# State-space layer: encoder product in three single passes, residual added by transfers, statistics and gates at other places

## The chip, the cores and the metric

One Trainium2 chip; the program runs on one of its cores. Its engines are TensorE (PE in the profile; PEld is its weight load), VectorE (DVE), ScalarE (ACT), GpSimd (POOL) and SyncE (SP), which here only issues transfers. The metric is the device time of one launch in microseconds: before the change 4286.31 us, the median of 3 runs (4282.78 to 4290.16).

## The reference

Four layers follow each other on x, 8 images of 384 channels by 32x32 points (1024 tokens). Each computes `x = x + layer(group_norm(x))`: attention, the state-space layer, a depthwise convolution, and a recurrent layer with a convolution. Only the second is changed. It computes, for each image:

```python
fx = layernorm(u, ln1_g, ln1_b)                   # u: group norm of x, tokens by channels
Bu = einsum('ph,blh->blp', B_bar, fx)             # complex, 192 states
xs = scan(lam_bar, Bu)                            # along the 1024 tokens
y  = 2*real(einsum('hp,blp->blh', Cc, xs)) + D*fx
y  = gelu(y) + fx
fy = layernorm(y, ln2_g, ln2_b)
z  = fy @ W_enc.T                                 # 384 -> 768, the encoder
z1, z2 = split(z)
y  = (z1 * gelu(z2)) @ W_dec.T + fy               # the decoder
x  = x + y
```

## The kernel before

`s5_layer` works on one image at a time, with the 384 channels as 3 tiles of 128 partitions and the 1024 tokens in two halves of 512 columns. Everything is float32. Its engines run three images deep: in turn `i` of the main loop they do the second layer norm, encoder and decoder of image `i`, the complex rotation, scan and back rotation of image `i+1`, and the group norm and first layer norm of image `i+2`. The order on each engine is the order in which its block is written (no planner), and engines meet at semaphores only. B is 8.

TensorE's order in a turn: group means of `i+2`; the products with `b_w` of `i+1` (18 matmuls of 128x128 by 128x512), between them the channel sums of the two layer norms (8 matmuls, `norm`); the second half of the decoder of image `i-1` (9); the encoder of `i` (`fill_enc`, L1515, 36); the first half of the decoder of `i` (L1526, 9); the products with `c_w` of `i+1` (`fill_c`, L1536, 18), which need the last of the nine rotations `turn_out` (L1362). All of these but the norm sums write into a ring of four PSUM banks (`ORDER`, `wait_for_bank`): a product waits until the reader of the product four places ahead has read. The encoder alternates a bank for gelu (read by ScalarE, `gates`, L1222) and a bank for the factor (read by VectorE, `apply_gate`, L1368, which multiplies it by the gate). So the fifth bank waits for gate 0, the sixth for `apply_gate(0)`, and so on; the ninth for gate 2.

VectorE in a turn, from the second layer norm's last step on: scale of `y` (`scale`, L853), end of the rotation `turn_in` (L1330 to L1334), second half of the outputs of image `i-1` (`outputs`: L1381 adds the decoder bank to `xres`, L1385 is its statistics), statistics of the input of image `i+3` (`moments`, L104), three scans (L1338) with the scale of `f` (L853) among them, nine `turn_out` (L1362), six `apply_gate` and two `add_residual` (L1373) among these, first half of the outputs of image `i`, then `activations` of `i+1` (L1411 and L1416), which take the banks of `c_w`.

ScalarE: the layer norm's gain and bias on `y` (`affine`, L1204), gates 0 and 1, gain and bias on `f` for image `i+2` (L1204 again), gates 2 to 5, the gelus of `activations`. GpSimd adds tiles for the first layer norm's sums (L1163 to L1171). `add_residual` adds the normalised `y` to `xres`, into which SP has loaded the layer's input of that image again (L1145); this load waits for the store of the image before from the same buffer.

A setup block ahead of the loop turns the weights by transposes on TensorE (L1064), which ScalarE copies out of PSUM (L976, L981, L984). All engines meet at its end, and the statistics of image 0 follow (L104).

Of the kernel before, what the change touches and what calls it, by code (L numbers as in the profile page):

```python
# [57 lines left out]
def as_f32(ap):  # L58
    return ap.bitcast(F32)
# [796 lines left out]
def s5_layer(nc, const, x_in, x_out, moments_out, w):  # L856
# [12 lines left out]
    with ExitStack() as ctx:  # L869
# [8 lines left out]
        enc_w = sb("enc_w", [P, CT, 2 * C])  # L878
# [7 lines left out]
        xres = sb("xres1", [P, CT, T])  # L886
        f1 = [sb(f"f1_{n}", [P, CT, T]) for n in range(2)]
        y = sb("y1", [P, CT, T])
        hid = sb("hid1", [P, CT, T])
# [10 lines left out]
        x_loaded, res_loaded, stored = (ctx.enter_context(nc.semaphore(n)) for n in ("x_loaded1", "res_loaded1", "stored1"))  # L900
# [11 lines left out]
        b_bar = flat(f1[0], 0, TILES * C).rearrange("p (k c) -> p k c", k=TILES)  # L912
        count, times, high, low, whole = u[:, 0, :].bitcast(mybir.dt.int32), u[:, 1, :], u[:, 2, :], u[:, 3, :], z[:, 0, :]
# [8 lines left out]
        with nc.cleanup_on_exit(), ExitStack() as setup:  # L922
            lam_loaded, b_loaded, c_loaded, w_loaded, params = (nc.alloc_semaphore(n) for n in (
                "lam_loaded", "b_loaded", "c_loaded", "w_loaded", "params"))
            counted, v, s, mixed, bar, turned, kept = (Signal(nc.alloc_semaphore(n)) for n in (
                "counted", "s5_v", "s5_s", "c_mixed", "b_barred", "turned1", "kept1"))
# [27 lines left out]
            def _(pool):  # L954
                pool.iota(count, pattern=[[1, T]], base=0, channel_multiplier=0).then_inc(counted.next(), 1)
                pool.wait_ge(c_loaded, 16)
                for part in range(2):
                    source = c_rows[:, :, 2 * P + part:2 * STATES:2]
                    pool.tensor_copy(c_mix[:, :, part * REST:(part + 1) * REST], source).then_inc(mixed.next(), 1)

            @block.scalar
            def _(act):
# [7 lines left out]
                for n in range(CT * 3 + TILES + CT):  # L970
                    act.wait_ge(turned.sem, turned.at(n + 1))
                    source = psum[:, n % RING, 0:C]
                    if n < CT * 3:
                        t, which = n // 3, n % 3
                        target = dec_w[:, t, :] if which == 2 else enc_w[:, t, which * C:(which + 1) * C]
# [104 lines left out]
        f_made = signal("f_made", 2 * CT)  # L1080
# [13 lines left out]
        res_added = signal("res_added", 2)  # L1094
# [35 lines left out]
        def _(sp):  # L1130
            def store(i):
                sp.wait_ge(out_made.sem, out_made.at(2 * CT, i))
                sp.dma_start(x_out[i:i + 1].rearrange("a (p t) n -> p (a t n)", t=CT), xres[:, :, :].rearrange("p t n -> p (t n)")).then_inc(stored, 16)

            for i in range(-3, B):
                if i == 0:
                    sp.dma_start(xres[:, :, :].rearrange("p t n -> p (t n)"), x_in[0:1].rearrange("a (p t) n -> p (a t n)", t=CT)).then_inc(res_loaded, 16)
# [36 lines left out]
        def _(act):  # L1174
# [49 lines left out]
            for i in range(-2, B):  # L1224
# [17 lines left out]
                if batch(i):  # L1242
                    gates(i, 0, 2)
# [1266 lines left out]
```

## Time and profile before

| | |
|---|---|
| median of the runs | 4286.31 us |
| the profiled execution | 4282.44 us |
| its span, first to last instruction | 4280.0 us |
| PE busy / DVE busy / ACT busy / POOL busy in the span | 91 / 72 / 53 / 32 % |
| one turn in the steady part of the layer (2265.30 to 2355.30 us) | 90.00 us |
| in that turn PE / DVE / ACT / POOL busy | 85.37 / 76.91 / 35.26 / 12.29 us |

The layer's setup begins at 1856.92 us and its last store is done by 2686.0 us. Times within the program are us from the start of the span. A row of the time line gives start, duration, engine, line, operation, tiles and count; a bracket at its end is the idle time ahead of it and who ended it. "fp32r" is the data type of the high and low parts with which TensorE does one pass over the moving columns; a float32 matmul appears as two instructions and is counted twice.

### The profile page before, as it was taken

The numbers are of one execution on the slowest core, as the hardware profiler recorded it, in microseconds if no ns is written. First come the engines' busy times: TensorE is split into PE (matmuls) and PEld (weight loads), VectorE is DVE, ScalarE is ACT, GpSimd is POOL, SyncE is SP. The second block draws the span as 40 slices with busy tenths as digits, with TensorE's granted clock in tenths as the row PEclk, the third lists the DMA queues.
The fourth block names the chain that finished last, engine by engine and source line by source line (L and its number), as shares of the span: only waits on it lengthen the run. The fifth ranks groups of instructions, "written<-read, shape, count | busy, mean of one in ns | idle before, by whom it ended". The sixth has DMA issues, their size and how long they took to land. (4 is left out here: it accounts for less than half of the span.)

```text
span 4280.0 us, 53507 instructions
## 1 busy us (share of the span) xinstructions
PE 3884.5 (91%) x17085; PEld 2311.0 (54%) x17085; DVE 3078.0 (72%) x3127; ACT 2283.8 (53%) x3634; POOL 1372.1 (32%) x1106
## 2 busy tenths in 40 slices
PE   6999999999999999946999999465999999999999
PEld 5777768686868677622444444243444444444444
DVE  4767676666767675557887885355878878878878
ACT  2867667676858585834433432212644644644644
POOL 2857666675757485822111100222000000000000
PEclk8999999999999999967999999687999999999999
DMA  4323333342423232221111111776010010010010
GB/s 125 84 85 96 98 88 106 81 111 74 115 79 104 79 105 73 54 76 49 54 49 50 49 53 46 195 207 203 4 44 16 29 44 16 28 44 16 28 44 15
DMA packets 115528, 312.07 MB, mean 73 GB/s; under 512 B 47890, under 2 KB 49506, under 8 KB 105586
## 3 DMA queue, kind: packets, MB, share of 16 engines
q1 hardware_dynamic: 106802, 276.75, 21.2%
q0 software_dynamic: 7504, 24.80, 2.3%
q10 hardware_dynamic: 1008, 7.67, 0.5%
q8 instruction: 134, 2.20, 0.2%
q14 instruction: 80, 0.66, 0.1%
HBM read 203.12 MB, written 101.30 MB: 71 GB/s over the span
## 5 line engine op out<-in xcount | busy, mean ns | idle before, releaser
L417 POOL TENSOR_TENSOR probs_lo<-probs,probs_hi 128x512 fp32r<-128x512 f32 x848 | 1169.4, 1394 | 639.7 <-ACT probs L463 618.5
L530 DVE TENSOR_REDUCE maxima<-m_psum 128x1 fp32r<-128x1024 f32 x512 | 625.5, 1222 | 371.7 <-PE m_psum L706 370.8
L462 ACT ACTIVATE probs_hi<-s_psum 128x512 fp32r<-128x512 f32 x1024 | 613.4, 599 | 383.5 <-PE o_psum L735 221.9
L2431 PE MATMUL psum<-mixes,last_weights 128*128 128x512 f32 x1728 | 751.2, 593 | 0.0
L463 ACT ACTIVATE probs<-s_psum 128x512 f32<-128x512 f32 x1024 | 609.0, 595 | 0.0
L2431 PEld LDWEIGHTS psum<-mixes,last_weights 128*128 128x128 f32 x1728 | 328.2, 190 | 409.1 <-issue 409.1
L719 PE MATMUL s_psum<-q_all,k_hi 128*128 128x512 f32 x1024 | 430.9, 421 | 26.0 <-ACT probs L463 25.7
L735 PE MATMUL o_psum<-probs_lo,v 128*112 128x512 f32 x1024 | 412.5, 403 | 12.6 <-DVE probs_lo L610 6.5
L720 PE MATMUL s_psum<-q_all,k_lo 128*128 128x512 f32 x1024 | 405.0, 396 | 0.0
L730 PE MATMUL o_psum<-probs_hi,v 128*112 128x512 f32 x1024 | 404.6, 395 | 0.0
L2438 PE MATMUL psum<-xp,last_weights 128*128 128x512 f32 x864 | 383.2, 597 | 18.4 <-DVEq L2315 13.3
L706 PE MATMUL m_psum<-k_hi,q_all 128*128 128x512 f32 x1024 | 342.8, 417 | 31.2 <-DVE maxima L530 18.0
L706 PEld LDWEIGHTS m_psum<-k_hi,q_all 128*128 128x128 f32 x1024 | 289.3, 324 | 73.7 <-DVE maxima L530 26.3
L2438 PEld LDWEIGHTS psum<-xp,last_weights 128*128 128x128 f32 x864 | 161.9, 189 | 233.7 <-issue 207.4
L1515 PE MATMUL psum<-y,enc_w 128*128 128x512 f32 x576 | 253.6, 600 | 13.2 <-DVE hid L1368 13.2
L719 PEld LDWEIGHTS s_psum<-q_all,k_hi 128*128 128x128 f32 x1024 | 195.7, 191 | 120.9 <-ACT probs L463 97.4
L1906 PE MATMUL psum<-xt,last_weights 32*32 32x248 f32 (+3 forms) x5376 | 134.3, 451 | 111.3 <-issue 79.9
L735 PEld LDWEIGHTS o_psum<-probs_lo,v 128*112 128x112 f32 x1024 | 180.2, 176 | 88.6 <-POOL probs_lo L417 21.2
L720 PEld LDWEIGHTS s_psum<-q_all,k_lo 128*128 128x128 f32 x1024 | 194.4, 190 | 25.7
L610 DVE TENSOR_TENSOR probs_lo<-probs,probs_hi 128x512 fp32r<-128x512 f32 x176 | 193.0, 1097 | 20.1 <-ACT probs L463 18.8
L730 PEld LDWEIGHTS o_psum<-probs_hi,v 128*112 128x112 f32 x1024 | 180.0, 176 | 45.4
L1515 PEld LDWEIGHTS psum<-y,enc_w 128*128 128x128 f32 x576 | 110.3, 193 | 155.9 <-issue 132.6
(329 smaller groups left out, 5941.0 us busy)
## 6 DMA issues: line engine op xcount, KB each, us to landing
xin<-x SPq DMA_DIRECT2D x17, 1536.0 KB, 6.7
xin<-in_x SPq DMA_DIRECT2D x16, 1536.0 KB, 7.4
k_hi<-k_rows_hi SPq DMA_DIRECT2D x128, 192.0 KB, 3.4
xres<-x SPq DMA_DIRECT2D x16, 1536.0 KB, 7.2
k_rows_hi<-stage_hi SPq DMA_DIRECT2D x48, 256.0 KB, 2.1
k_rows_lo<-stage_lo SPq DMA_DIRECT2D x48, 256.0 KB, 2.3
q_rows_hi<-stage_hi SPq DMA_DIRECT2D x48, 256.0 KB, 2.4
q_rows_lo<-stage_lo SPq DMA_DIRECT2D x48, 256.0 KB, 2.5
```

The costliest lines, as they stand in the source:

```text
L417: pool.tensor_tensor(probs_lo[:, u % RING, :], probs[:, u % RING, :], as_f32(probs_hi[:, u % RING, :]), ALU.subtract).then_inc(pool_low.ne ...
L462: nc.scalar.activation(probs_hi[:, u % RING, :], s_psum[:, u % 2, :], ACT.Exp, scale=SCALE)
L463: nc.scalar.activation(probs[:, u % RING, :], s_psum[:, u % 2, :], ACT.Exp, scale=SCALE).then_inc(exped.next(), 1)
L530: nc.vector.tensor_reduce(maxima[:, g % 2, tile:tile + 1], source, AX.X, ALU.max, negate=True).then_inc(rows_max.next(), 1)
L706: ins = nc.tensor.matmul(pair_of(other)[:, half, :], q_all[:, g % SLOTS, tile::KEYS], k_hi[:, g % SLOTS, cols_of(half)], start=True, stop= ...
L719: nc.tensor.matmul(s_psum[:, u % 2, :], k_hi[:, h % SLOTS, keys], q, start=True, stop=False)
L720: nc.tensor.matmul(s_psum[:, u % 2, :], k_lo[:, h % SLOTS, keys], q, start=False, stop=True).then_inc(scored.next(), 1)
L730: nc.tensor.matmul(o_psum[0:USED, half, :], v[:, tile, h, :], probs_hi[:, u % RING, :], start=(tile == 0), stop=False)
L735: nc.tensor.matmul(o_psum[0:USED, half, :], v[:, tile, h, :], probs_lo[:, u % RING, :], start=False, stop=(tile == KEYS - 1)).then_inc(wei ...
L1515: ins = nc.tensor.matmul(bank("enc", i, 2 * n + k), enc_w[:, t, first + m * P:first + (m + 1) * P], y[:, t, cols(half)], start=(t == 0), s ...
L2431: ins = nc.tensor.matmul(bank, conv_w[:, t, down, factor, m * P:(m + 1) * P], mixes[:, factor, t, down:down + S, :].rearrange("p a b -> p ...
L2438: ins = nc.tensor.matmul(bank.rearrange("p (a b) -> p a b", b=S), weights[:, t, m * P:(m + 1) * P], rows_of(t, half), start=(t == 0), stop ...
```

## The change

Three things are done in `s5_layer`, and nothing elsewhere.

The encoder's operands are split. In the setup GpSimd makes from the turned weights a high part (a copy that rounds to fp32r) and a low part (the difference), six pieces of 128x384 each. For each image ScalarE writes gain and bias of `y` into `y_hi` (`highs`, in place of the first `affine`), and `y_lo` is the difference of the full value and `y_hi` (`lows`, VectorE). The full value itself is written into `residuals[i % 2]`: half 0 by VectorE, half 1 by ScalarE (`wholes`). Each float32 matmul of the encoder becomes three fp32r ones: high by high, low weights by high, high weights by low.

The residual has two buffers now. The load of the layer's input into `xres` and both `add_residual` are gone; GpSimd, once all of `y_lo` is made, issues three transfers that add the input of the image onto the full value in SBUF, and `outputs` waits for them.

The order is another: the six statistics of the next input image are spread over the first three `outputs` and the first three `activations`, with their total behind; the six `apply_gate` stand between other instructions than before.

```diff
+                for t in range(CT):
+                    for which in range(2):
+                        at = enc_turned[:, t, which * C:(which + 1) * C]
+                        high, low = (w_part[:, t, which * C:(which + 1) * C] for w_part in (enc_hi, enc_lo))
+                        pool.wait_ge(kept.sem, kept.at(3 * t + which + 1))
+                        pool.tensor_copy(high, at).then_inc(enc_split.next(), 1)
+                        pool.wait_ge(enc_split.sem, enc_split.at(enc_split.count))
+                        pool.tensor_tensor(low, at, as_f32(high), ALU.subtract).then_inc(enc_split.next(), 1)
...
-                    sp.wait_ge(out_measured.sem, out_measured.at(1, i - 1))
-                    sp.wait_ge(stored, 16 * i)
-                    sp.dma_start(xres[:, :, :].rearrange("p t n -> p (t n)"), x_in[i:i + 1].rearrange("a (p t) n -> p (a t n)", t=CT)).then_inc(res_loaded, 16)
...
+                if batch(i):
+                    pool.wait_ge(low_made.sem, low_made.at(2 * CT, i))
+                    for t in range(CT):
+                        pool.dma_start(residuals[i % 2][:, t, :], x_in[i].rearrange("(p t) n -> p t n", t=CT)[:, t, :],
+                                       accum_op=ALU.add).then_inc(res_added, 16)
...
+            def wholes(i):
...
+                for t in range(CT):
+                    nc.scalar.activation(residuals[i % 2][:, t, cols(1)], y[:, t, cols(1)], ACT.Identity,
+                                         scale=rows["ln2_g"][:, t:t + 1], bias=rows["ln2_b"][:, t:t + 1]).then_inc(f_second_half.next(), 1)
...
-                    affine(y, rows["ln2_g"], rows["ln2_b"], scaled2, f_made, i)
+                    highs(i)
...
-                    gates(i, 0, 2)
+                    gates(i, 0, 1)
+                    wholes(i)
+                    gates(i, 1, 2)
...
+            def lows(i, half):
+                whole = residuals[i % 2]
+                if half == 0:
...
+                    for t in range(CT):
+                        nc.vector.tensor_scalar(whole[:, t, cols(0)], y[:, t, cols(0)], rows["ln2_g"][:, t:t + 1], rows["ln2_b"][:, t:t + 1],
+                                                ALU.mult, ALU.add).then_inc(f_first_half.next(), 1)
+                for t in range(CT):
...
+                    dve.wait_ge(high_made.sem, high_made.at(nth, i))
+                    nc.vector.tensor_tensor(y_lo[:, t, cols(half)], whole[:, t, cols(half)], as_f32(y_hi[:, t, cols(half)]),
+                                            ALU.subtract).then_inc(low_made.next(), 1)
...
                         for t in range(CT):
-                            ins = nc.tensor.matmul(bank("enc", i, 2 * n + k), enc_w[:, t, first + m * P:first + (m + 1) * P],
-                                                   y[:, t, cols(half)], start=(t == 0), stop=(t == CT - 1))
+                            for w_part in (enc_hi, enc_lo):
+                                nc.tensor.matmul(bank("enc", i, 2 * n + k), w_part[:, t, at], y_hi[:, t, cols(half)],
+                                                 start=(t == 0 and w_part is enc_hi), stop=False)
+                        for t in range(CT):
+                            if m == 0 and k == 0:
+                                pe.wait_ge(low_made.sem, low_made.at(CT * half + t + 1, i))
+                            ins = nc.tensor.matmul(bank("enc", i, 2 * n + k), enc_hi[:, t, at], y_lo[:, t, cols(half)],
+                                                   start=False, stop=(t == CT - 1))
```

VectorE in a steady turn, from the outputs of the image before to the third gate; `hid` is `apply_gate`, `z<-decay,u` a scan. Before:

```order
668 L1393 SCALAR_TENSOR_TENSOR x_moments<-x_moments 128x1
669 L104 BN_STATS gn_stats<-xin 128x6 x6
...
672 L1338 SCALAR_TENSOR_TENSOR z<-decay,u 128x1024
673 L853 TENSOR_TENSOR f_1<-f_1,ln_inv 128x3x512 x2
674 L1368 TENSOR_TENSOR hid<-gate,psum 128x512
675 L1338 SCALAR_TENSOR_TENSOR z<-decay,u 128x1024 x2
676 L1368 TENSOR_TENSOR hid<-gate,psum 128x512
```

And now:

```order
764 L1449 SCALAR_TENSOR_TENSOR x_moments<-x_moments 128x1
765 L1425 TENSOR_TENSOR hid<-gate,psum 128x512
766 L1395 SCALAR_TENSOR_TENSOR z<-decay,u 128x1024
767 L1333 TENSOR_TENSOR y_lo<-xres_0,y_hi 128x512 x3
768 L1425 TENSOR_TENSOR hid<-gate,psum 128x512
769 L853 TENSOR_TENSOR f_0<-f_0,ln_inv 128x3x512 x2
770 L1425 TENSOR_TENSOR hid<-gate,psum 128x512
771 L1395 SCALAR_TENSOR_TENSOR z<-decay,u 128x1024
```

The statistics are gone from here, the first gate stands ahead of the first scan, and the third stands directly behind the scale of `f` instead of behind two more scans and four rotations.

ScalarE at the same place; `y_hi` and `y` are gain and bias of the second norm, `f` those of the first. Before:

```order
814 L1204 ACTIVATE y<-y,ln_b_c,ln_g_c 128x512 x6
...
817 L1222 ACT_TABLE_LOAD
818 L1222 ACTIVATE gate<-psum 128x512 x2
819 L1204 ACTIVATE f_1<-f_1,ln_b_c,ln_g_c 128x512 x6
820 L1222 ACTIVATE gate<-psum 128x512 x4
```

And now:

```order
835 L1228 ACTIVATE y_hi<-y,ln_b_c,ln_g_c 128x512 x6
...
839 L1254 ACTIVATE gate<-psum 128x512
840 L1236 ACTIVATE xres_0<-y,ln_b_c,ln_g_c 128x512 x3
841 L1254 ACTIVATE gate<-psum 128x512
842 L1219 ACTIVATE f_0<-f_0,ln_b_c,ln_g_c 128x512 x6
843 L1254 ACTIVATE gate<-psum 128x512 x4
```

Three activations stand between the first two gates; the third gate is behind the six of `f`, as before.

## Rows read from the trace of the kernel before

**Rows 1.** Windows, one steady turn: us; PE, PEld, DVE, ACT, POOL; PEclk, DMA, GB/s.

```profile
2265.30:2355.30 90.00, 85.37 (x201) 37.27 (x199) 76.91 (x93) 35.26 (x47) 12.29 (x8) 1.00 0.16 59
```

**Rows 2.** Time line of PE in that turn, from encoder to c_w products.

```profile
2297.10 13.04 PE L1515 MATMUL psum<-y,enc_w 128*128 128x512 f32 x30
2312.84 15.72 PE L1515 MATMUL psum<-y,enc_w 128*128 128x512 f32 x36 [2.70 <-DVE hid L1368]
2329.34 2.84 PE L1515 MATMUL psum<-y,enc_w 128*128 128x512 f32 x6 [0.78 <-DVE hid L1368]
2332.02 7.89 PE L1526 MATMUL psum<-hid,dec_w 128*128 128x512 f32 x18
2339.75 15.61 PE L1536 MATMUL psum<-u,c_w 128*128 128x512 f32 x36
```

**Rows 3.** Time line of PE in the attention layer: fp32r matmuls, one each.

```profile
1002.15 0.39 PE L720 MATMUL s_psum<-q_all,k_lo 128*128 128x512 f32 x1
1002.37 0.39 PE L730 MATMUL o_psum<-probs_hi,v 128*112 128x512 f32 x1
```

**Rows 4.** Time line of DVE in the turn of rows 1.

```profile
2291.31 4.97 DVE L853 TENSOR_TENSOR y<-y,ln_inv 128x1536 f32<-128x1536 f32 x2
2296.20 0.68 DVE L1330 TENSOR_TENSOR prod<-u,tables 128x512 f32<-128x512 f32 x1
2298.01 1.27 DVE L1381 TENSOR_TENSOR xres<-xres,psum 128x512 f32<-128x512 f32 x2
2302.30 3.65 DVE L104 BATCH_NORM_STATS2 gn_stats<-xin 128x6 f32<-128x512 f32 x6
2308.79 3.40 DVE L853 TENSOR_TENSOR f<-f,ln_inv 128x1536 f32<-128x1536 f32 x2
2312.11 0.68 DVE L1368 TENSOR_TENSOR hid<-gate,psum 128x512 f32<-128x512 f32 x1
2312.70 4.47 DVE L1338 TENSOR_TENSOR_SCAN z<-decay,u 128x1024 f32<-128x1024 f32 x2
2327.47 1.23 DVE L1362 TENSOR_TENSOR u<-u 128x1024 f32<-128x1024 f32 x1
2328.61 0.68 DVE L1368 TENSOR_TENSOR hid<-gate,psum 128x512 f32<-128x512 f32 x1
```

**Rows 5.** Time line of ACT in the same turn.

```profile
2310.56 4.34 ACT L1204 ACTIVATE f<-f,ln_b_c,ln_g_c 128x512 f32<-128x512 f32 x6 [4.93 <-DVE f L853]
2314.80 0.57 ACT L1222 ACTIVATE gate<-psum 128x512 f32<-128x512 f32 x1
```

**Rows 6.** Time line of DVE: a tensor_scalar while it builds its tables.

```profile
1896.28 0.69 DVE L1298 TENSOR_SCALAR u<-u 128x1024 f32<-128x1024 f32 x1
```

**Rows 7.** Time line of PE: encoder and c_w products of images 5 and 7.

```profile
2476.99 31.06 PE L1515 MATMUL psum<-y,enc_w 128*128 128x512 f32 x72
2515.61 15.61 PE L1536 MATMUL psum<-u,c_w 128*128 128x512 f32 x36
2633.35 31.06 PE L1515 MATMUL psum<-y,enc_w 128*128 128x512 f32 x72
```

**Rows 8.** Time line at the end of the setup.

```profile
1871.80 1.10 POOL L959 COPY xres<-xres 128x192 f32<-128x192 f32 x2 [13.88 <-DMA xres<-in_L_conv_Cmat]
1875.65 1.24 ACT L984 COPY b_w<-psum 128x384 f32<-128x384 f32 x3 [0.96 <-PE psum L1064]
1878.41 3.66 DVE L104 BATCH_NORM_STATS2 gn_stats<-xin 128x6 f32<-128x512 f32 x6 [3.53 <-PEq L922]
```

**Rows 9.** Groups of the page and of POOL: busy us, mean ns, idle ahead.

```profile
L610 DVE TENSOR_TENSOR probs_lo<-probs,probs_hi 128x512 fp32r<-128x512 f32 x176 | 193.0, 1097 | 20.1 <-ACT probs L463 18.8
L1163 POOL TENSOR_TENSOR first_sums<-f 128x512 f32<-128x512 f32 x16 | 21.3, 1329 | 439.3 <-ACT f L1182 439.3
```

**Rows 10.** Page, part 6: issues, KB each, median us to landing.

```profile
xres<-x SPq DMA_DIRECT2D x16, 1536.0 KB, 7.2
dw_res<-x POOLq DMA_DIRECT2D x96, 128.0 KB, 4.1
```

More of the change, by code:

```diff
@@ L877, in s5_layer @@
         c_w = sb("c_w", [P, TILES, C])
-        enc_w = sb("enc_w", [P, CT, 2 * C])
+        enc_hi, enc_lo = (sb(f"enc_w_{part}", [P, CT, 2 * C], F32R) for part in ("hi", "lo"))
         dec_w = sb("dec_w", [P, CT, C])
@@ L974, in _ @@
                         t, which = n // 3, n % 3
-                        target = dec_w[:, t, :] if which == 2 else enc_w[:, t, which * C:(which + 1) * C]
+                        target = dec_w[:, t, :] if which == 2 else enc_turned[:, t, which * C:(which + 1) * C]
                         nc.scalar.copy(target, source).then_inc(kept.next(), 1)
@@ L1407, in activations @@
                 for n in range(2 * CT + 2):
+                    if i >= 1 and batch(i + 2):
+                        if n < CT:
+                            measure(i + 2, CT + n)
+                        if n == CT + 1:
+                            moments(i + 2)
                     if n < 2 * CT:
@@ L1436, in _, with scale_and_split @@
                     table(1)
-                scale_second = (lambda: scale(norm2, y, inv_made2, scaled2, i)) if here else None
+                def scale_and_split():
+                    scale(norm2, y, inv_made2, scaled2, i)
+                    lows(i, 0)
+                scale_second = scale_and_split if here else None
                 if after:
@@ L1443, in _ @@
                     outputs(i - 1, EARLY, 2 * CT)
-                if batch(i + 3):
+                if batch(i + 3) and not here:
+                    for n in range(2 * CT):
+                        measure(i + 3, n)
                     moments(i + 3)
+                if here:
+                    apply_gate(i, 0)
                 if after:
                     scan(i + 1, 0)
+                if here:
+                    lows(i, 1)
+                    apply_gate(i, 1)
                 if third:
@@ L1450, in _ @@
                 if here:
-                    apply_gate(i, 0)
+                    apply_gate(i, 2)
                 if after:
                     scan(i + 1, 1)
+                if here:
+                    apply_gate(i, 3)
+                if after:
                     scan(i + 1, 2)
-                if here:
-                    apply_gate(i, 1)
-                if after:
-                    for n in range(4):
+                    for n in range(2):
                         turn_out(i + 1, n)
                 if here:
-                    apply_gate(i, 2)
+                    apply_gate(i, 4)
+                if after:
+                    for n in range(2, 4):
+                        turn_out(i + 1, n)
+                if here:
+                    apply_gate(i, 5)
                 if after:
```

67 lines of the change are left out of this document (45 added, 22 removed).

## The prediction

> **What bounds the kernel now.** I read the windows of the layer first, then the time lines of TensorE, VectorE and ScalarE in one turn, and last the rows of the setup. A steady turn lasts 90.0 us; TensorE is busy for 85.37 of it at full clock, VectorE for 76.91, ScalarE for 35.26 [rows 1]. TensorE is the bound, with 5 us of gaps, of which 2.70 and 0.78 are waits in the encoder for `apply_gate` on VectorE [rows 2]. So two things could shorten a turn: less work on TensorE, and gates that come earlier. VectorE is only 8.5 us behind and gets more work, so I follow both engines through the turn until the products with `c_w` start (2339.75 us before). These need the last rotation of VectorE, and what follows them is as before. The turn is shorter by what this start gains.
>
> **TensorE's part.** The encoder's 36 float32 matmuls are 72 instructions, 31.06 us where nothing waits [rows 7], so 0.863 us for each matmul. Now there are 108 fp32r ones. In the attention layer these start 0.22 to 0.23 us apart, each with its own weights [rows 3]; with 0.231 the encoder takes 24.95 us, 6.1 less. This is a size that the trace shows for the same kind of operation, so I keep its other bounds narrow: 0.215 to 0.25, 23.2 to 27 us. After it come 9 decoder matmuls, 7.73 us (2332.02 to 2339.75, [rows 2]). From the start of the encoder, 2297.10, TensorE alone would reach the `c_w` products after 33 us at 2330, against 2339.75.
>
> **VectorE's part.** I count from the end of the scale of `y`, 2296.20 [rows 4], in the new order. An operation on 128x512 takes 0.59 us from start to start (2312.11 to 2312.70), a rotation 1.14 (2327.47 to 2328.61), a scan 2.2 (4.47 for two), the scale of `f` 3.35, the second half of the outputs with its total 4.3 (2298.01 to 2302.30) [rows 4]. A `tensor_scalar` on 128x1024 takes 0.69 [rows 6], so three on 512 about 1.2.
>
> Low parts of half 0: 1.2 + 3x0.6 + 0.1 for waiting on itself = 3.1, to 2299.3. End of `turn_in` 1.8, outputs 4.3, gate 0 0.6, scan 2.2, low parts of half 1 1.8, gate 1 0.6, scale of `f` 3.35: 2313.95. Now gate 2 is due, and there is the new wait. ScalarE makes this gate behind its six activations on `f`, and these wait for the scale of `f`. Before, the scale ended at 2312.1 (VectorE went on at 2312.11) and the gate at 2315.4 [rows 4, 5]: 3.3 us later, which nobody felt, since `apply_gate(2)` came far behind. It now stands directly behind the scale, so VectorE waits 3.3 us, to 2317.25. Queued behind it are all that follows: gate 2 0.6, scan 2.2, gate 3 0.6, scan 2.2, two rotations 2.27, gate 4 0.6, two rotations 2.27, gate 5 0.6, five rotations 5.75. The last rotation ends at 2334.35.
>
> TensorE beside it: its first low-part matmul waits until 2298.1, the third until 2299.3, which costs 0.3; the ninth bank needs gate 2, is due at 2314.1 and starts at 2317.4, 3.3 us lost; the others find their gates done, since gate 0 (2306.0) and gate 1 (2310.7) are now ahead of the banks that need them (2308.4 and 2312). The 2.70 and 0.78 of before are gone. The encoder ends at 2325.6, the decoder's half at 2333.4, and TensorE waits a microsecond for the rotation. So the start is 2334.35 instead of 2339.75: **5.4 us per steady turn**, set by VectorE. This holds for images 1 to 4: 21.6 us.
>
> The statistics (six times 0.61, before all in one piece of 3.65 and with their total 4.3 us [rows 4]) cost nothing at their new place: three lie among the first outputs and three in `activations`. From 2334.35 VectorE has 9 operations (5.4 us), then 3 statistics, the total, five products and the sums, together 14.2 us in the 15.61 us of the `c_w` products. Beyond 1.4 us more the next turn would begin late by the rest. The two additions of the residual (2 x 1.67 us between the last gates) are gone as well; they are simply not in the new chain.
>
> **The other images.** Image 0 has no earlier outputs (4.3 less on VectorE), image 6 no scale of `f` and no wait for gate 2 (6.65 less): there TensorE is the bound and gains about 5.9 each. Image 7 has nothing behind its encoder but the decoder: 6.0. Image 5 had no input statistics before, so its encoder ran without a wait, 38.62 us from its start to the `c_w` products [rows 7]; the new chain is the same as above, 37.25 us, gain 1.4. Together 21.6 + 11.8 + 6.0 + 1.4 = 40.8 us.
>
> **The setup.** GpSimd was done with two copies at 1872.9, and the block ended with `b_w` at 1876.9; the statistics start 1.5 later [rows 8]. Now GpSimd has twelve more instructions on 128x384 that start at 1872.9, because the weights come out earlier. A subtraction on 128x512 takes 1.33 us on it [rows 9], so 0.97 on 384. A copy isn't shown in this size: 0.55 for 192 columns [rows 8] gives 0.55 at least and 1.1 at most. I take 0.8, between them, and 0.1 for each of the twelve waits: 6x(0.97 + 0.8) + 1.2 = 11.8, end 1884.7, **8 us late**, all on the path, since every engine meets there. Bounds 6 and 10.
>
> **The transfers.** The old load of 1536 KB took 7.2 us from issue to landing [rows 10]; it and its wait for the store go and nothing was waiting there. The new ones start when the low parts are complete (2310.0) and are wanted at 2334.35: 24.3 us. No row shows a transfer that adds. From below: as a plain one, 7 us, hidden. From above: three times that, 21.6, still hidden in a steady turn; image 6 has only 17.7 us (4 us lost), image 7 some 20.7. I take it as hidden, nearest to the plain row; GpSimd has nothing else to do behind the issue until the next turn.
>
> The Trainium skill, "SBUF — State Buffer", section "SBUF: two separate sides", says that a transfer issued by GpSimd stands still while VectorE runs an operation that takes both of its ports, because GpSimd can't write the descriptors; "Who interferes with whom" there names `tensor_scalar` as such and `tensor_tensor` as not. By that the new issue would be undisturbed, as the only `tensor_scalar` of a turn lie 12 us ahead of it; if the rule held for the other operations too, the issue would wait up to one of them. No run here shows it yet.
>
> **Sum.** 4282.44 - 40.8 + 8 = 4249.6 for the profiled execution; this one lay 3.9 us under the median, so 4253.5 as a median, 32.7 us or 0.8% faster.
>
> **Rivals.**
> 1. *No wait at gate 2.* If ScalarE has the gate early, VectorE reaches the last rotation at 2331.05, TensorE is at 2330.2, and the turn gains 8.7: 34.8 for four images, 4.7 for image 5, 17.8 for the rest, less 8: 4237. For it: 35 of 90 us busy on ScalarE. Against it: its order, in which gate 2 follows the activations on `f`.
> 2. *VectorE pays more for the low parts.* The same kind of subtraction has a mean of 1097 ns in the attention layer, where GpSimd works beside it [rows 9], instead of 0.6. Six of them cost 3 us a turn, and image 1 to 5 lose that from the chain, 15 us: 4269. Against it: GpSimd is idle in this stretch.
> 3. *Transfers that land late* (the other side). VectorE stands at the first output, and TensorE behind it as its banks stay full. With landing L after the last low part, six images lose L - 24.3, image 6 L - 17.7 and image 7 L - 20.7. The 32.7 us are used up at L = 27.1, nearly four times the plain load; at 30 us the loss is 55.8 and the kernel takes 4309. For it: an adding transfer has to read its target, and rows of such a kind are missing. Against it: it would have to go at 50 KB/us where the plain load goes at 213.
> 4. *The gain is eaten.* Setup 10 instead of 8, fp32r matmuls at 0.25, low parts dearer and 4 us lost at image 6: 4280, no measurable change.
>
> **Chances.** My forecast with its own spread (4246 to 4262) 0.55, rival 1 0.12, rival 2 0.14, rival 3 0.07, rival 4 0.12, of which a part is still faster. What a measurement of this kernel can tell from no change is about 0.2%, 8.6 us: faster means under 4277.7. That gives 0.85 faster (0.55, 0.12, 0.14 and a third of rival 4's), 0.08 the same, 0.07 slower. Range 4236 to 4280: from rival 1 to rival 4, all but rival 3 and a little at either end.
>
> **What would show it.** In the new profile: the encoder's fp32r matmuls 0.23 us apart; a wait of VectorE of about 3.3 us for gate 2, released by ScalarE, and TensorE's wait of the same size in front of the ninth bank; turns of 84.6 us; `c_w` products that wait about a microsecond for a rotation; GpSimd's copies and subtractions to 1885 and the statistics of image 0 at about 1886.4; no wait of VectorE for a transfer at the first output. A turn of 81 would speak for rival 1, a turn of 88 or subtractions of over 0.7 for rival 2, an idle time ahead of the first output released by a DMA for rival 3.

## The result and the profile after

The changed kernel took 4251.73 us (median of 4 runs, 4245.56 to 4256.85) beside 4288.21 us for the kernel before (4 runs): a ratio of 0.9919, 95% interval 0.9906 to 0.9933 (the medians divided by each other give 0.9915). The forecast was 4253.5, in a range of 4236 to 4280. The profiled execution took 4248.17 us with a span of 4246.4, against 4282.44 and 4280.0.

To see where the time went I use two marks that both traces have: the start of a row of `c_w` products (once a turn), and the whole distance of the layer from the first GpSimd instruction of its setup (an IOTA) to the first matmul on `x_moments` behind its last image. First these marks in the trace after; columns: start in us, busy us, engine, line, operation, tiles, count, and in brackets the idle time ahead with what ended it.

```profile
1858.75 0.98 POOL L961 IOTA u<- 128x1024 int32 x1 [27.41 <-POOLq L181]
1986.48 17.10 PE L1615 MATMUL psum<-u,c_w 128*128 128x512 f32 x36 [19.75 <-DVE u L1419]
...
2241.06 15.72 PE L1615 MATMUL psum<-u,c_w 128*128 128x512 f32 x36 [1.00 <-DVE u L1419]
2326.43 15.72 PE L1615 MATMUL psum<-u,c_w 128*128 128x512 f32 x36 [1.00 <-DVE u L1419]
2411.79 15.72 PE L1615 MATMUL psum<-u,c_w 128*128 128x512 f32 x36 [1.01 <-DVE u L1419]
2497.13 15.72 PE L1615 MATMUL psum<-u,c_w 128*128 128x512 f32 x36 [1.01 <-DVE u L1419]
2573.42 15.61 PE L1615 MATMUL psum<-u,c_w 128*128 128x512 f32 x36
...
2657.08 0.58 PE L1968 MATMUL psum<-x_moments,group_mean 128*128 128x16 f32 x2 [6.20 <-PEq L869]
```

The layer takes 2657.08 - 1858.75 = 798.3 us. Before, its marks stood at 1856.94 and 2686.12, 829.2 us. So it gained **30.9 us**; the prediction had 40.8 - 8 = 32.8. The rest of the program, which the change doesn't touch, took 3450.8 us in the trace before and 3448.1 in the trace after. Over all twelve profiled executions of this case it lies between 3448.1 and 3456.2 with no visible relation to the kernel. So single times here differ by some microseconds for reasons outside the layer, the medians lie 36.5 us apart where the layer gained 30.9, and part of the closeness of 4251.7 to 4253.5 is luck of that kind. Below, each term is judged by the marks.

The marks have a spread too, as each kernel has one trace. From the IOTA to the first `c_w` products the seven kernels that split the weights in the setup have as good as the same code and take 127.7 to 129.3 us. The first `c_w` products stand behind a wait of some 20 us, TensorE does part of them at its lower clock, and they take 17.1 to 18.8 us over the twelve kernels. So layers that differ by 3 us or less are told apart by their turns, which repeat within 0.15 us, and not by the whole distance.

A steady turn is now 85.37 us. Windows of it (us; busy time and count of PE, PEld, DVE, ACT, POOL; granted clock; DMA share; GB/s), which answers to [rows 1]:

```profile
2241.06:2326.43 85.37, 81.17 (x235) 44.83 (x235) 78.13 (x100) 37.27 (x50) 14.90 (x11) 0.98 0.22 62
```

TensorE is busy 4.2 us less than in [rows 1], not 6.1, and its clock is no longer whole. The time line of VectorE in this turn, which answers to [rows 4]:

```profile
2282.67 4.97 DVE L853 TENSOR_TENSOR y<-y,ln_inv 128x1536 f32<-128x1536 f32 x2
2287.56 1.45 DVE L1324 TENSOR_SCALAR xres<-y,ln_g_c,ln_b_c 128x512 f32<-128x512 f32 x3
2288.93 1.88 DVE L1333 TENSOR_TENSOR y_lo<-xres,y_hi 128x512 fp32r<-128x512 f32 x3
...
2292.55 1.27 DVE L1435 TENSOR_TENSOR xres<-xres,psum 128x512 f32<-128x512 f32 x2
...
2297.20 0.69 DVE L1425 TENSOR_TENSOR hid<-gate,psum 128x512 f32<-128x512 f32 x1 [0.28 <-PE psum L1594]
...
2302.39 3.42 DVE L853 TENSOR_TENSOR f<-f,ln_inv 128x1536 f32<-128x1536 f32 x2
2309.04 0.69 DVE L1425 TENSOR_TENSOR hid<-gate,psum 128x512 f32<-128x512 f32 x1 [3.23 <-ACT gate L1254]
...
2325.15 1.22 DVE L1419 TENSOR_TENSOR u<-u 128x1024 f32<-128x1024 f32 x1
2326.29 0.68 DVE L1435 TENSOR_TENSOR xres<-xres,psum 128x512 f32<-128x512 f32 x1
```

The wait at gate 2 is there, 3.23 us, and ScalarE releases it. The first output at 2326.29 waits for no transfer. ScalarE shows why the gate comes so late, as in [rows 5]: its six activations on `f` run first.

```profile
2304.18 4.35 ACT L1219 ACTIVATE f<-f,ln_b_c,ln_g_c 128x512 f32<-128x512 f32 x6 [4.38 <-DVE f L853]
2308.43 1.06 ACT L1254 ACTIVATE gate<-psum 128x512 f32<-128x512 f32 x2
```

And TensorE, which answers to [rows 2]:

```profile
2289.84 1.53 PE L1594 MATMUL psum<-y_lo,enc_w_hi 128*128 128x512 f32 x3
2293.27 0.79 PE L1589 MATMUL psum<-y_hi,enc_w_hi 128*128 128x512 f32 x1 [1.90 <-DVE xres L1435]
2293.86 0.63 PE L1589 MATMUL psum<-y_hi,enc_w_lo 128*128 128x512 f32 x1
2294.29 0.63 PE L1589 MATMUL psum<-y_hi,enc_w_hi 128*128 128x512 f32 x1
...
2297.16 0.40 PE L1589 MATMUL psum<-y_hi,enc_w_lo 128*128 128x512 f32 x1
2297.40 0.39 PE L1589 MATMUL psum<-y_hi,enc_w_hi 128*128 128x512 f32 x1
```

Here stand two things that the prediction did not have. In front of the second encoder bank TensorE waits 1.90 us for VectorE's addition of an output (L1435): this bank is the one that the decoder of the image before still holds, and the addition that frees it now stands behind the low parts: 5.0 us behind the end of the scale of `y`, where it stood 1.8 behind it [rows 4]. And behind this wait the fp32r matmuls start 0.43 us apart instead of 0.23, until 2296.9: the granted clock is 0.73 over the 6 us from 2293.27, so the engine runs at its lower level (1.2 GHz) for part of them.

The setup, which answers to [rows 8]:

```profile
1873.45 1.00 POOL L965 COPY xres<-xres 128x192 f32<-128x192 f32 x2 [13.72 <-DMA xres<-in_L_conv_Cmat]
1874.40 0.65 POOL L971 CAST enc_w_hi<-z 128x384 fp32r<-128x384 f32 x1
1875.13 1.18 POOL L973 TENSOR_TENSOR enc_w_lo<-z,enc_w_hi 128x384 fp32r<-128x384 f32 x1
...
1882.68 0.50 POOL L971 CAST enc_w_hi<-z 128x384 fp32r<-128x384 f32 x1
1883.26 0.99 POOL L973 TENSOR_TENSOR enc_w_lo<-z,enc_w_hi 128x384 fp32r<-128x384 f32 x1
1885.11 3.66 DVE L104 BATCH_NORM_STATS2 gn_stats<-xin 128x6 f32<-128x512 f32 x6 [7.80 <-PEq L928]
```

From the IOTA to the first statistics it is 26.36 us against 21.47 before: 4.9 us, not 8.

### The profile page after: what moved, and what is told of

It reads as the page before. It is cut to its first block and busy times, and to the rows that moved or that the text cites. A ratio compares the mean times of both kernels' runs of the same rounds, so it can differ in the third digit from the quotient of the medians.

```text
span 4246.4 us, 54195 instructions
## 1 busy us (share of the span) xinstructions
PE 3846.9 (91%) x17373; PEld 2366.5 (56%) x17373; DVE 3092.6 (73%) x3183; ACT 2300.1 (54%) x3658; POOL 1402.0 (33%) x1142
## 5 line engine op out<-in xcount | busy, mean ns | idle before, releaser
L706 PE MATMUL m_psum<-k_hi,q_all 128*128 128x512 f32 x1024 | 343.1, 417 | 30.9 <-DVE maxima L530 18.1
L1985 PE MATMUL psum<-xt,last_weights 32*32 32x240 f32 (+3 forms) x5376 | 136.1, 456 | 108.3 <-issue 74.5
L610 DVE TENSOR_TENSOR probs_lo<-probs,probs_hi 128x512 fp32r<-128x512 f32 x176 | 193.2, 1098 | 20.1 <-ACT probs L463 18.8
L1985 PEld LDWEIGHTS psum<-xt,last_weights 32*32 32x32 f32 x5376 | 95.2, 115 | 148.9 <-issue 97.9
L790 PE MATMUL m_psum<-heads,proj_w 128*128 128x512 f32 x384 | 166.8, 594 | 8.7 <-DVE v L536 8.7
```

The lines of the kernel that those rows point to most:

```text
L706: ins = nc.tensor.matmul(pair_of(other)[:, half, :], q_all[:, g % SLOTS, tile::KEYS], k_hi[:, g % SLOTS, cols_of(half)], start=True, stop= ...
L1985: ins = nc.tensor.matmul(out[:, :, rows], bands[q * S:(q + 1) * S, g, channel, tap, 0:S], xt[q * S:(q + 1) * S, t % 2, g * GROUP + channel ...
```

## The experiments

Ten kernels ran, in three groups; each group has its own runs of the kernel before (4284.92 us for the first four, 4285.14 for the next four, 4287.44 for the last two), and the ratio is to these; that of the changed kernel is to 4288.21. "Layer" is the distance between the two marks above in the one profiled execution, which leaves out what varies elsewhere.

```
kernel                       median us  ratio to before [95%]      layer us  steady turn
before                                                             829.2     89.9
changed kernel               4251.73    0.9919 [0.9906, 0.9933]    798.3     85.4
order_only                   4269.50    0.9962 [0.9948, 0.9976]    817.7     86.6
split_only                   4310.16    1.0061 [1.0044, 1.0077]    857.5     96.0
two_pass                     4241.33    0.9892 [0.9875, 0.9908]    783.9     85.0
no_residual                  4250.91    0.9916 [0.9899, 0.9932]    800.0     85.4
gate2_early                  4237.50    0.9888 [0.9872, 0.9905]    785.8     82.6 or 84.2
add_early                    4248.25    0.9911 [0.9894, 0.9927]    796.7     85.2
late_split                   4246.29    0.9907 [0.9891, 0.9924]    792.8     85.0
both                         4233.41    0.9879 [0.9863, 0.9896]    779.6     82.2
best                         4230.45    0.9866 [0.9850, 0.9881]    775.0     82.2
best_stats                   4221.10    0.9848 [0.9834, 0.9861]    767.0     81.0
```

### The change in its parts

**order_only** is the kernel before with VectorE's new order alone: three statistics among the first outputs and three in `activations`, and gates 0 to 5 at their new places. It keeps the loaded residual, whose two additions move behind the last rotation. Of its edit, the first three gates:

```diff
+                if here:
+                    apply_gate(i, 0)
                 if after:
                     scan(i + 1, 0)
+                if here:
+                    apply_gate(i, 1)
...
                 if here:
-                    apply_gate(i, 0)
+                    apply_gate(i, 2)
```

> The kernel before with two parts of the change alone: the statistics of the next input spread over outputs and activations, and the six gates at their new places; float32 encoder, loaded residual (its two additions stand behind the last rotation). My theory: TensorE still takes 31.06 us for the encoder and 7.73 for the decoder's half, but waits for no gate any more, so a steady turn falls from 90.0 by the 3.5 us of waits to about 86.5, image 5 gains nothing, and the whole is 12 to 16 us faster than before (ratio about 0.997). VectorE will still wait some 3 us for gate 2 behind the activations on f, without a price, because TensorE is the later of the two. Rival: the order is worth nothing by itself and the gain is all the fp32r encoder's: turns of 90, ratio 1.000.

Turns of 86.56 us (`c_w` products at 2243.5, 2330.1 and 2416.7), TensorE busy for 85.07 of 86.60 us. The order takes the encoder's waits away, and TensorE, with its float32 encoder, is then the bound. That is 11.5 us of the layer (15.4 by the medians), and with 1.5 us of gaps left in a turn little more can come from the order alone. VectorE's wait for gate 2 is there as well, 3.21 us, and costs nothing, as expected.

**split_only** is the changed kernel with the old order (statistics in one piece, gate 0 behind the scale of `f`).

```diff
-                if here:
-                    apply_gate(i, 0)
                 if after:
                     scan(i + 1, 0)
                 if here:
                     lows(i, 1)
-                    apply_gate(i, 1)
...
                 if here:
-                    apply_gate(i, 2)
+                    apply_gate(i, 0)
```

> The changed kernel with the order of VectorE undone: statistics in one piece ahead of the first scan and the gates at their old places (low parts of half 1 behind the first scan); split encoder and adding transfers kept. My theory: VectorE's longer chain and late gates hold the encoder's banks, the encoder ends about 10 us later than in the changed kernel, and a steady turn takes 93 to 95 us, more than the 90.0 of before; the whole is 10 to 25 us slower than before (ratio 1.002 to 1.006). Rival: TensorE's saving of 6.1 us a turn counts whatever the order: turns of 84 to 86 and a ratio near 0.991.

Turns of 96.0 us, the layer 28.3 us slower than before, although its encoder matmuls are the faster ones. TensorE's time line shows where they stand:

```profile
2227.77 0.50 PE L1578 MATMUL psum<-y_hi,enc_w_hi 128*128 128x512 f32 x1 [1.91 <-DVE xres L1435]
...
2243.68 0.80 PE L1578 MATMUL psum<-y_hi,enc_w_hi 128*128 128x512 f32 x1 [7.39 <-DVE hid L1425]
```

A faster encoder fills its banks sooner and then waits 7.39 us for gate 0. That alone explains no loss against the kernel before. But the split also puts the low parts on VectorE ahead of this gate: it starts 20.9 us behind the end of the scale of `y`, where it started 15.9 behind it [rows 4], and these 5.0 us are most of the 6 by which the turn got longer. The turn is longer than the 93 to 95 us that I expected. So the two parts are not additive: -11.5 for the order, +28.3 for the split, together -30.9. The split needs the order; the order brings something by itself.

**two_pass** leaves out the product of the low part of the weights with the high part of `y`.

```diff
-                            for w_part in (enc_hi, enc_lo):
+                            for w_part in (enc_hi,):
```

> The changed kernel without the products of the weights' low part (they are left out of the encoder): 72 instead of 108 fp32r matmuls, 8.3 us less for TensorE per image. My theory: VectorE's chain sets the turn, so steady turns stay at 85.4 less at most 1, images 6 and 7 gain some 2 and 8, in all 10 to 16 us less than the changed kernel (ratio to before about 0.989). Rival: TensorE is the bound and the turn falls by 8.3: 60 us less (ratio 0.978).

A third of the encoder's work gone from TensorE, 8.3 us, and the steady turn is 0.4 us shorter. TensorE just waits longer, 3.80 us instead of nothing at gate 2:

```profile
2305.71 0.69 DVE L1425 TENSOR_TENSOR hid<-gate,psum 128x512 f32<-128x512 f32 x1 [3.22 <-ACT gate L1254]
2305.73 1.65 PE L1589 MATMUL psum<-y_hi,enc_w_hi 128*128 128x512 f32 x3 [3.80 <-ACT gate L1254]
...
2323.09 2.41 PE L1615 MATMUL psum<-u,c_w 128*128 128x512 f32 x5 [1.14 <-DVE u L1419]
```

Of the gain, 14.4 us of the layer, images 6 and 7 bring 4.3 and 8.3: there TensorE is the bound. This shows that VectorE's chain sets the steady turns of the changed kernel, as predicted.

**no_residual** leaves out the three accumulating transfers and VectorE's wait for them.

```diff
-                if batch(i):
-                    pool.wait_ge(low_made.sem, low_made.at(2 * CT, i))
-                    for t in range(CT):
-                        pool.dma_start(residuals[i % 2][:, t, :], ..., accum_op=ALU.add).then_inc(res_added, 16)
...
-                        if n == 0:
-                            dve.wait_ge(res_added, 16 * CT * (i + 1))
```

> The changed kernel without the three adding transfers and without the wait for them (the layer's input is left out of its output). Theory: they land 10 us after the low parts are complete, 14 us before they are wanted, and cost nothing: the time of the changed kernel within 3 us (ratio 0.992). Rival: their traffic slows the swap of the scans' third tile or GpSimd's port slows VectorE: over 5 us faster than the changed kernel.

4250.91 against 4251.73 us, the same turns to 0.05 us (the layers differ by 1.6 us the other way, 1.55 of it ahead of the first `c_w` products): the transfers are hidden. In the changed kernel they are issued behind the last low part and land in a median of 7.8 us (5.4 to 10.5 over the 24), while 24 us are there.

```profile
2302.17 2.63 POOL L1185 DMA_DIRECT2D xres<-x x3 [16.15 <-DVE y_lo L1333]
```

### The two waits

**gate2_early** puts ScalarE's gate 2 ahead of its six activations on `f`.

```diff
-                    gates(i, 1, 2)
+                    gates(i, 1, 3)
...
-                    gates(i, 2, 2 * CT)
+                    gates(i, 3, 2 * CT)
```

> Full computation. ScalarE evicts and activates gate 2 (index 2) of the image ahead of the six activations of f instead of behind them. My theory: of the 3.2 us that VectorE waits for that gate in each turn (2309.04 in the trace of the changed kernel), all but about 0.3 goes, but TensorE has lost time earlier in the turn (1.90 us waiting for the decoder bank before the second encoder bank, then 0.43 us instead of 0.22 per start for some microseconds) and is itself only 1.0 us ahead of its wait for u, so the scan chain can be pulled forward by at most about 1 us before the next turn's start is set by TensorE. Expected: turns 84.4 us against 85.4, about 4246 us, ratio to before 0.991, that is 3 to 7 us under the changed kernel. Rival (the wait at gate 2 is the only thing that bounds the turn): turns 82.5, about 4230 us. Rival (the wait only moves to another one of the VectorE chain): no change, 4252 us.

More than my theory gave: 785.8 us for the layer, 12.5 less than the changed kernel. The wait at gate 2 is down to 0.43 us, as expected:

```profile
2298.17 0.69 DVE L1425 TENSOR_TENSOR hid<-gate,psum 128x512 f32<-128x512 f32 x1 [0.43 <-ACT gate L1254]
```

But the turns come in two lengths, and the rows of the windows tell why:

```profile
2146.43:2230.64 84.21, 81.02 (x235) 45.06 (x234) 78.78 (x101) 37.28 (x50) 14.92 (x11) 0.98 0.23 63
2230.64:2313.27 82.63, 79.44 (x235) 43.90 (x234) 77.76 (x100) 37.39 (x50) 14.92 (x11) 1.00 0.23 64
2313.27:2395.91 82.64, 79.44 (x236) 43.89 (x235) 78.19 (x101) 37.40 (x50) 14.91 (x11) 1.00 0.23 64
2395.91:2480.11 84.20, 81.03 (x236) 45.02 (x234) 78.75 (x101) 37.27 (x50) 14.90 (x11) 0.98 0.18 44
```

In the turns of 84.2 us the granted clock is 0.98 and TensorE busy for 81.0 us, in those of 82.6 it is 1.00 and 79.4. The wait in front of the second encoder bank is in all of them. The time line of TensorE in a long and in a short turn:

```profile
2198.55 0.50 PE L1589 MATMUL psum<-y_hi,enc_w_hi 128*128 128x512 f32 x1 [1.90 <-DVE xres L1435]
...
2201.86 0.63 PE L1589 MATMUL psum<-y_hi,enc_w_lo 128*128 128x512 f32 x1
2202.28 0.63 PE L1589 MATMUL psum<-y_hi,enc_w_hi 128*128 128x512 f32 x1
...
2282.77 0.50 PE L1589 MATMUL psum<-y_hi,enc_w_hi 128*128 128x512 f32 x1 [1.90 <-DVE xres L1435]
2283.10 0.40 PE L1589 MATMUL psum<-y_hi,enc_w_lo 128*128 128x512 f32 x1
2283.34 0.40 PE L1589 MATMUL psum<-y_hi,enc_w_hi 128*128 128x512 f32 x1
```

My 84.4 is near what the turns take in which the clock falls, and the error was to take the fall for granted. The same wait of 1.90 us is followed by it in two of these four turns, and this costs 1.6 us. The second rival, that the wait at gate 2 alone bounds the turn (82.5 us), came out for the others.

**add_early** takes the other wait away: the output addition that frees the second encoder bank moves ahead of the low parts of half 0, the two others right behind them. Not shown: `outputs` skips the three there.

```diff
                     scale(norm2, y, inv_made2, scaled2, i)
+                    if batch(i - 1):
+                        add_output(i - 1, EARLY)
                     lows(i, 0)
+                    if batch(i - 1):
+                        for n in range(EARLY + 1, 2 * CT):
+                            add_output(i - 1, n)
```

> Full computation. VectorE's three early output additions of the image before stand one ahead of the low parts of y and two right behind the first half of them, so that the decoder bank which the second encoder bank takes is free sooner; gate 2 stays behind f's activations. My theory: the 1.90 us wait of TensorE at the second encoder bank goes, and with it most of the stretch at half clock (0.43 us a start instead of 0.22); but gate 2 still comes behind the activations of f, so VectorE's chain to u keeps its length and TensorE waits some 2.5 us at the ninth bank or ahead of the matmul on u. Expected: turns 85.2 to 85.6 us, 4250 us, ratio 0.9915. Rival (TensorE's lost time bounds the turn by itself): turns 82.5, about 4231 us. Rival (the additions ahead lengthen the chain by 0.4 to 1.2 us): turns 86.2, 4257 us.

The wait at the second bank is gone, and the turn stays at 85.2 us, since the wait for gate 2 stays. TensorE now has a wait of its own for the same gate, and the lower clock follows there:

```profile
2304.45 0.69 DVE L1425 TENSOR_TENSOR hid<-gate,psum 128x512 f32<-128x512 f32 x1 [3.22 <-ACT gate L1254]
2304.47 0.73 PE L1600 MATMUL psum<-y_hi,enc_w_hi 128*128 128x512 f32 x1 [2.30 <-ACT gate L1254]
2304.99 0.63 PE L1600 MATMUL psum<-y_hi,enc_w_lo 128*128 128x512 f32 x1
2305.42 0.63 PE L1600 MATMUL psum<-y_hi,enc_w_hi 128*128 128x512 f32 x1
```

The layer is only 1.6 us shorter, but images 6 and 7, where TensorE is the bound, gain 1.6 us each; the stretch up to the first `c_w` products and these products took longer here, within the spread given above.

**both** has the two edits.

> Full computation. Both edits: gate 2 ahead of the activations of f on ScalarE, and the early output additions spread around the low parts on VectorE. My theory: each of the two waits hides the other (3.2 us of VectorE at gate 2; 1.9 us plus the half-clock stretch of TensorE at the second encoder bank), so only together do they give their full time. Expected: turns 82.0 to 82.6 us against 85.4, six of them, about 4234 us, ratio 0.988. Rival (gains are additive, no hiding): the sum of the two single gains, thus 4244 us or more if each gives 1 to 4 us. Rival (something third is 1 us behind, such as ScalarE's evictions): turns 84, 4243 us.

Turns of 82.22 us and a layer of 779.6, 18.7 us less than the changed kernel, where the single edits give 12.5 and 1.6. From the second `c_w` products on, without the stretch that varies, it is 17.9 against 11.2 and 4.3: 2.4 more than their sum, and the two falls of the clock in gate2_early are 3.2 us. Neither engine waits inside the encoder for longer than 0.5 us, and the clock is whole in the steady turns:

```profile
2232.76:2314.98 82.22, 79.69 (x234) 43.80 (x234) 78.06 (x100) 37.16 (x50) 14.91 (x11) 1.00 0.23 64
```

My theory, that each wait hides the other, holds only one way. Taking away TensorE's wait alone gives nearly nothing, since VectorE sets the turn; taking away VectorE's alone gives most of it, up to where TensorE becomes the bound. What the second edit adds is 0.4 us in the turns with the full clock and 2.0 us in the others.

### The setup, and what beats both kernels

**late_split** makes the encoder weights' high and low parts in the main loop, by GpSimd beside the scan work of the first image, instead of in the setup. The turned weights lie in `residuals[1]` instead of `z` for it, and TensorE waits for the parts ahead of the first encoder.

```diff
+                if i == -1:
+                    pool.wait_ge(turned_out.sem, turned_out.at(TURNS_OUT, 0))
+                    for t in range(CT):
+                        ... (tensor_copy to enc_hi, tensor_tensor to enc_lo)
```

> Full computation. The encoder weights' high and low parts are made by GpSimd in the main loop, beside the scan work of the first image, instead of in the setup; nothing else changes. My theory: the setup's 4.9 us over the kernel before (IOTA to first statistics 26.36 against 21.47 us) goes and nothing in the loop waits for the split. Expected: about 4246.5 us, ratio 0.9905, turns still 85.4. Rival (GpSimd's twelve instructions, 9.9 us, slow VectorE or delay the residual transfers of that turn): gain under 2 us, 4250 us. Rival (the setup's longer distance is due to something else, such as the order of loads): no gain, 4252 us.

The first statistics start at 1879.30, 21.41 us behind the IOTA at 1857.89: the 4.9 us are gone, and the loop has room for the work. The two kernels below that have this edit show 21.4 us as well, and the seven with the split in the setup 26.4 to 27.7. The layer is 5.5 us shorter. Its first turn is 1.3 us longer (85.03 against 83.71), all of it in its first `c_w` products (18.44 against 17.10 us, the spread given above). Its other turns are 0.4 us shorter. TensorE has the same wait of 1.90 us at the second bank in them, but full clock behind it in four of the five, and in the other one the clock falls 1.3 us later than in the changed kernel. A steady turn and its second bank:

```profile
2235.76:2320.75 84.99, 79.98 (x235) 43.72 (x235) 78.04 (x100) 37.27 (x50) 14.89 (x11) 1.00 0.22 62
...
2287.97 0.50 PE L1593 MATMUL psum<-y_hi,enc_w_hi 128*128 128x512 f32 x1 [1.90 <-DVE xres L1437]
2288.31 0.39 PE L1593 MATMUL psum<-y_hi,enc_w_lo 128*128 128x512 f32 x1
```

So the second bank is full in time, and VectorE has no wait at gate 0 in any of them, where it waits 0.25 to 0.37 us in the changed kernel.

**best** is both with late_split.

> Full computation. Gate 2 ahead of the activations of f, early output additions spread around the low parts, and the encoder weights' split in the main loop. My theory: the three gains stand in different places (VectorE's wait at gate 2, TensorE's wait at the second encoder bank with the half-clock stretch behind it, the setup) and so add: turns 82.2 us as in the kernel with the two waits gone, and some 5 us less of setup. Expected 4228 us, ratio to before 0.9867. Rival (the split on GpSimd now stands in a turn that has no idle time left to hide it, 9.9 us): 4233 to 4238 us.

4230.45 us, 2.5 above what I wrote; the layer is 775.0 us, 4.6 below that of `both`, with the same turns. The setup's gain adds to the others, as it stands in a different place.

**best_stats** moves VectorE's three late statistics and their aggregate (2.4 us) from the place ahead of gate 0 to behind the last rotation; the edit is against the kernel `best`.

```diff
-                if batch(i - 1):
-                    outputs(i - 1, EARLY, 2 * CT)
...
+                if batch(i - 1):
+                    outputs(i - 1, EARLY, 2 * CT)
                 if here:
                     outputs(i, 0, early(i))
```

> Full computation. As the kernel above, and VectorE's three late statistics of the image before with their aggregate (2.4 us) stand behind the last rotation instead of ahead of the first gate. My theory: the 82.2 us turn is bounded by VectorE's chain to u; taking 2.4 us out of it gives back no more than TensorE's 0.9 us wait before the matmuls on u, less what the 2.4 us cost behind it, where the additions to y wait only 1.7 us in all for TensorE. Expected: turns 81.5 to 82.0 us, 4225 us. Rival (the chain alone counts): turns 79.8, 4213 us. Rival (the statistics now delay y and the sums behind it): turns 82.9, 4232 us.

4221.10 us, the fastest here: 1.5% under the kernel before. The turn is 81.03 us, 1.2 shorter: below the 81.5 to 82.0 that I expected, and a little more than the 0.9 us that TensorE had waited. The `c_w` products now start without a wait. TensorE waits 1.4 us in a turn (1.15 in the decoder's second half, 0.26 for a low part) and is the bound again:

```profile
2223.70 15.61 PE L1630 MATMUL psum<-u,c_w 128*128 128x512 f32 x36
2304.73 15.61 PE L1630 MATMUL psum<-u,c_w 128*128 128x512 f32 x36
```

## Why the prediction was right, and where not

*The mechanism of the steady turn held.* VectorE's chain sets the turn, as two_pass shows (8.3 us less work for TensorE shorten it by 0.4), with the wait for gate 2 in it (3.3 us predicted, 3.23 measured) and with `c_w` products that wait about a microsecond (1.00). The matmuls start 0.23 us apart where the clock is whole. The chain from the end of the scale of `y` to the end of the last rotation was to be 38.15 us and is 38.7 (2287.56 to 2326.29): the gate 0 wait of 0.28, 0.2 for three `tensor_scalar` of 0.46 rather than 0.4 each, and small change. TensorE starts 0.14 behind the rotation, and the stretch ahead of the scale is 0.1 longer (41.61 instead of 41.50). Together the turn is 85.37, not 84.6: 4.5, 5.2, 4.6 and 4.6 us for images 1 to 4 where 5.4 each were forecast, 2.7 us too much in all.

*The step that failed* is "TensorE beside it: its first low-part matmul waits until 2298.1 [...] the ninth bank needs gate 2, is due at 2314.1". I followed the encoder's banks to the gates that free them, and not to the outputs of the image before. The second bank waits 1.90 us for such an output, which the low parts had pushed back by 3.2 us. With the lower clock behind it this used up the time that TensorE would have waited at the ninth bank: no wait is left there. In the steady turn this costs little beyond the 0.28 us at gate 0, since VectorE's chain is as long: add_early, which takes the wait away, has turns of 85.2, and late_split, in whose steady turns the wait is there but the clock stays whole, 85.0. In image 6, where TensorE is the bound, it has its price: 1.23 us of wait in the trace, and a gain of 4.6 us instead of 5.9. There the clock stays whole (1.00).

*The other images.* Image 0 gained 5.5 (5.9 forecast), of which 0.8 us lie in its first `c_w` products (17.10 instead of 17.86 us), where it is the spread given above and not the change. Image 5 gained 0.6 (1.4), image 7 6.0 (6.0). With images 1 to 4 and image 6 that is 35.5 us for 40.8.

*The setup* was a term of the right kind and a wrong size: 8 forecast, 4.9 measured. A copy of 384 columns takes 0.50 to 0.65 us where I took 0.8, the twelve instructions 9.85 us instead of 11.8, and the statistics begin 0.86 us behind the block's last instruction, not 1.5. late_split shows that all of the 4.9 us came from them. This error (3.1 us) and those of the images (5.3) had opposite signs, and that the sum came out within 2 us of the layer's gain is luck.

*The transfers* are hidden, as no_residual shows by leaving them out. By the Trainium skill, "SBUF — State Buffer", section "SBUF: two separate sides", GpSimd can't write the descriptors of a transfer while VectorE runs an operation in a mode that takes both ports. The trace agrees as far as it goes: the three issues take 2.63 us beside the scale of `f`, a `tensor_tensor`, which the prediction took for none of these, and no less, 2.62 and 2.60 us, in images 6 and 7, where no such scale runs and VectorE is idle for more than half of the time. The `tensor_scalar` of the turn lie 13 us ahead, so the other half of the rule isn't tested here.

*The rivals.* Rival 1 (no wait at gate 2) is what gate2_early builds, and it comes to 4237.5 us where I had reckoned 4237, though with the smaller setup and the wait at the second bank, which I didn't know, in it. Rival 2 fell: a low part takes 0.6 us. Rival 3 fell with no_residual. In rival 4 one part was near: the image terms came out smaller, but the setup did too.

What stays open: why the clock falls behind the 1.90 us wait in all five turns of the changed kernel that have it, but only in two of five of gate2_early, and in one of five each of late_split and split_only.

## What to carry to other kernels

When a step moves in the order of an engine, follow everything that is pushed back by it to whoever waits for it, the banks that the image before still holds included: a bank has two users. A faster matmul pays only if the engine that empties its banks comes earlier as well, and the work that the faster form puts on that engine counts; here the split without the new order lost 28 us, and with it won 31. Once a turn is bound by a chain through three engines, read its waits in order and take away the one that the bounding engine itself shows (gate 2 on VectorE), then the next, until no engine but one waits; with the split out of the setup that was worth as much again as the change (31.4 us of the layer).

## What the runs showed of the hardware

Three accumulating transfers of 512 KB from GpSimd's queue land in 5.4 to 10.5 us each, side by side, where the plain one of 1536 KB took 7.2 [rows 10]. A copy from float32 to fp32r of 128x384 on GpSimd takes 0.50 to 0.65 us, hardly more than the copy of 192 columns (0.50 in the same trace); a subtraction of 128x384 takes 0.99 to 1.21, where I had 0.97 from one of 512 columns. An fp32r matmul of 128x512 starts each 0.23 us at full clock and each 0.43 at the lower level. After a wait of 1.90 us in the midst of the encoder, TensorE ran at the lower level in some turns (granted clock 0.72 to 0.74 over the 6 us behind it) and at the full one in others (1.00), with no difference in its own instructions within one kernel. Over the six kernels that have this wait it was 20 turns of 31; behind waits of 1.2 us in the same place (image 6 of five of these kernels) it was none. A pause of about 2 us must thus be reckoned with and without 1.6 us on top.
